# Attention on one core: score and output tiles made in pairs, their matmuls in turn

## What is computed

```
xn = group_norm(x, gamma, beta)              # 16 images, N = 1024 tokens, C = 512
q = xn @ wq + bq;  k = xn @ wk + bk;  v = xn @ wv + bv
scores = einsum('bnc,bmc->bnm', q, k) * C ** -0.5
attn = softmax(scores)
out = einsum('bnm,bmc->bnc', attn, v) @ wp + bp + x
```

## Time and profile before

| | |
|---|---|
| median of 3 runs | 2161.06 us (2159.78 to 2163.63) |
| profiled execution | 2159.59 us, of which the trace's span is 2157.9 us |
| TensorE matmul busy | 2137.5 us, 99%, 9425 instructions |
| TensorE weight loads | 1765.7 us, 82% |
| VectorE / ScalarE / POOL busy | 1454.1 (67%) / 673.8 (31%) / 826.9 us (38%) |
| mean granted TensorE clock | 0.997 |
| DMA | 106.03 MB, 49 GB/s |

### The profile page before, as it was taken

How to read it: one execution, slowest core, us unless ns; L and a number is a source line. 1 busy time by engine, 2 the same in 40 slices (tenths; PEclk the granted TensorE clock), 3 DMA queues, 4 the chain that set the end, 5 groups by cost and what they waited for, 6 DMA issues and landing times.

```text
span 2157.9 us, 28171 instructions
## 1 busy us (share of the span) xinstructions
PE 2137.5 (99%) x9425; PEld 1765.7 (82%) x9425; DVE 1454.1 (67%) x2280; ACT 673.8 (31%) x1113; POOL 826.9 (38%) x487
## 2 busy tenths in 40 slices
PE   7999999999999999999999999999999999999998
PEld 5888888888888888888888888888888888888886
DVE  6776675857768476784856758576684767847454
ACT  3241332414233132331413324142331323314231
POOL 4344343433433334333443434334333343324433
PEclk9999999999999999999999999999999999999999
DMA  7003021130302103021030210303021030210201
GB/s 171 20 16 102 1 74 44 34 83 0 97 20 58 58 5 102 10 63 53 10 107 0 73 44 32 85 0 96 21 58 59 5 102 10 63 53 10 69 0 59
DMA packets 109260, 106.03 MB, mean 49 GB/s; under 512 B 8493, under 2 KB 74033, under 8 KB 109233
## 3 DMA queue, kind: packets, MB, share of 16 engines
q1 hardware_dynamic: 109184, 105.68, 17.4%
q10 hardware_dynamic: 48, 0.01, 0.0%
HBM read 72.10 MB, written 33.55 MB: 49 GB/s over the span
## 4 chain that ended last, share of the span: by engine, by line
PE 96%; POOL 1%; SPq 1%; issue 1%; DMA 1%; DVE 0%; ACT 0%; DVEq 0%; POOLq 0%; ACTq 0%
PE psum L790 21%; PE psum L792 21%; PE psum L791 21%; PE psum L873 11%; PE psum L874 11%; PE psum L875 11%; SPq L236 1%; DMA w_p<-in_L_conv_wp_dram 1%; POOL bias_part L372 0%; SPq L251 0%; POOL out_bias L376 0%; PE psum L836 0%; POOL out_bias L378 0%; DVE pt_lo L526 0%; ACT wv_t_hi L471 0%
## 5 line engine op out<-in xcount | busy, mean ns | idle before, releaser
L873 PE MATMUL psum<-v_hi,pt_hi 128*128 128x512 f32 x1024 | 400.0, 391 | 2.6 <-DVE pt_lo L526 2.5
L790 PE MATMUL psum<-t_hi,xn_hi 128*128 128x512 f32 x1024 | 399.9, 391 | 0.4 <-DVE v_lo L526 0.4
L874 PE MATMUL psum<-v_lo,pt_hi 128*128 128x512 f32 x1024 | 399.3, 390 | 0.0
L875 PE MATMUL psum<-v_hi,pt_lo 128*128 128x512 f32 x1024 | 399.2, 390 | 0.0
L792 PE MATMUL psum<-t_hi,xn_lo 128*128 128x512 f32 x1024 | 398.5, 389 | 0.0
L791 PE MATMUL psum<-t_lo,xn_hi 128*128 128x512 f32 x1024 | 398.5, 389 | 0.0
L324 POOL TENSOR_TENSOR x_res<-x_res,out_bias 128x512 f32<-128x512 f32 (+1 forms) x144 | 181.6, 1271 | 419.7 <-issue 232.0
L618 DVE TENSOR_TENSOR top_part<-top_part,score 128x512 f32<-128x512 f32 x192 | 169.6, 883 | 235.4 <-ACT score L453 234.1
L346 POOL TENSOR_TENSOR total_part<-total_part,score 128x512 f32<-128x512 f32 x192 | 280.7, 1462 | 47.4 <-ACT score L458 32.8
L453 ACT ACTIVATE score<-psum 128x512 f32<-128x512 f32 x256 | 151.5, 600 | 460.8 <-PE psum L792 460.8
L458 ACT ACTIVATE score<-score 128x512 f32<-128x512 f32 x256 | 157.9, 633 | 305.0 <-DVE score L634 305.0
(11 more groups left out here) (101 smaller groups left out, 3004.3 us busy)
## 6 DMA issues: line engine op xcount, KB each, us to landing
x_res<-in_x_dram SPq DMA_DIRECT2D x128, 256.0 KB, 2.8
out_dram<-x_res SPq DMA_DIRECT2D x128, 256.0 KB, 2.1
x_blk<-in_x_dram SPq DMA_DIRECT2D x240, 128.0 KB, 2.9
score<-in_x_dram SPq DMA_DIRECT2D x16, 128.0 KB, 7.6
w_q<-in_L_conv_wq_dram SPq DMA_DIRECT2D x4, 256.0 KB, 4.3
w_k<-in_L_conv_wk_dram SPq DMA_DIRECT2D x4, 256.0 KB, 7.0
w_v<-in_L_conv_wv_dram SPq DMA_DIRECT2D x4, 256.0 KB, 7.9
w_p<-in_L_conv_wp_dram SPq DMA_DIRECT2D x1, 1024.0 KB, 11.0
```

Source lines behind the costliest of these rows:

```text
L790: nc.tensor.matmul(dst, s_hi_, m_hi_, start=n == 0, stop=False)
L873: nc.tensor.matmul(dst, pt_hi[:, m, queries], v_hi[:, m, :], start=m == 0, stop=False)
L874: nc.tensor.matmul(dst, pt_hi[:, m, queries], v_lo[:, m, :], start=False, stop=False)
L875: last = nc.tensor.matmul(dst, pt_lo[:, m, queries], v_hi[:, m, :], start=False, stop=m == NT - 1)
```

## The change

Score tiles m and m + 1 are made together, and so are output tiles i and i + 1. Within a pair each matmul of the one is followed by the same matmul of the other: same moving operand, other weights, other bank. Both banks are waited for ahead of the pair's first matmul, and one signal after its last reports both tiles. An output pair waits for the `tile_out` that frees its second bank. The second group sum still stands behind s(1,1). Nothing changes on the other engines.

```diff
@@ -792,6 +792,17 @@
                     last = nc.tensor.matmul(dst, s_lo_, m_hi_, start=False, stop=n == len(pairs) - 1)
                 return last
 
+            def two_products(dsts, pairs):
+
+                steps = len(pairs[0])
+                for n in range(steps):
+                    for parts in range(3):
+                        for dst, own in zip(dsts, pairs):
+                            s_hi_, s_lo_, m_hi_, m_lo_ = own[n]
+                            last = nc.tensor.matmul(dst, s_lo_ if parts == 2 else s_hi_, m_lo_ if parts == 1 else m_hi_,
+                                                    start=n == 0 and parts == 0, stop=n == steps - 1 and parts == 2)
+                return last
+
             def chunk(c):
                 return slice(c * P, (c + 1) * P)
 
@@ -846,34 +857,34 @@
                 product(dst, [(xn_hi[:, k, chunk(m)], xn_lo[:, k, chunk(m)], m_hi[:, k, :], m_lo[:, k, :])
                               for k in range(KC)]).then_inc(s_work, 1)
 
-            def score_tile(n, h, m):
+            def score_tiles(n, h, m):
                 if m == 0:
 
                     pe.wait_ge(s_free, n * SPLIT + PLACE[("t", h, KC - 1)] + 1)
-                dst = work_bank(n, "s", h, m)
-                product(dst, [(xn_hi[:, k, chunk(m)], xn_lo[:, k, chunk(m)], t_hi[:, k, :], t_lo[:, k, :])
-                              for k in range(KC)]).then_inc(s_work, 1)
-
-            def out_tile(n, i, more):
+                dsts = [work_bank(n, "s", h, m), work_bank(n, "s", h, m + 1)]
+                two_products(dsts, [[(xn_hi[:, k, chunk(c)], xn_lo[:, k, chunk(c)], t_hi[:, k, :], t_lo[:, k, :])
+                                     for k in range(KC)] for c in (m, m + 1)]).then_inc(s_work, 2)
+
+            def out_tiles(n, i, more):
                 h = i // TH
                 if i == 0:
 
                     pe.wait_ge(s_free, (n + 1) * SPLIT)
                 if i >= TH or not starts(n):
 
-                    pe.wait_ge(s_y, n * NT + i - TH + 1)
-                if i == TH - 1 and more:
+                    pe.wait_ge(s_y, n * NT + i + 1 - TH + 1)
+                if i == TH - 2 and more:
 
                     pe.wait_ge(s_pw_in, n + 2)
-                dst = o_ps[i % TH]
                 for m in range(NT):
                     if i % TH == 0:
                         pe.wait_ge(s_ptl, (n * NH + h) * NT + m + 1)
-                    queries = chunk(i % TH)
-                    nc.tensor.matmul(dst, pt_hi[:, m, queries], v_hi[:, m, :], start=m == 0, stop=False)
-                    nc.tensor.matmul(dst, pt_hi[:, m, queries], v_lo[:, m, :], start=False, stop=False)
-                    last = nc.tensor.matmul(dst, pt_lo[:, m, queries], v_hi[:, m, :], start=False, stop=m == NT - 1)
-                last.then_inc(s_o, 1)
+                    for weights, moving in ((pt_hi, v_hi), (pt_hi, v_lo), (pt_lo, v_hi)):
+                        for c in (i, i + 1):
+                            last = nc.tensor.matmul(o_ps[c % TH], weights[:, m, chunk(c % TH)], moving[:, m, :],
+                                                    start=m == 0 and moving is v_hi and weights is pt_hi,
+                                                    stop=m == NT - 1 and weights is pt_lo)
+                last.then_inc(s_o, 2)
 
             pe.wait_ge(s_const, 6)
             weight_transpose(SET_WQ, w_q, s_wload[0])
@@ -898,8 +909,8 @@
             def image(b, more):
                 v_tile(b, 0)
                 v_tile(b, 1)
-                for m in range(NT):
-                    score_tile(b, 0, m)
+                for m in range(0, NT, 2):
+                    score_tiles(b, 0, m)
                 for j in range(KC):
                     t_chunk(b, 1, j)
                 for m in range(2, NT):
@@ -907,17 +918,17 @@
                     if more:
                         if m == 3:
                             group_sum(b + 1, 0, mv[:, :, 0])
-                for m in range(NT):
-                    score_tile(b, 1, m)
-                    if more and m == 1:
+                for m in range(0, NT, 2):
+                    score_tiles(b, 1, m)
+                    if more and m == 0:
                         group_sum(b + 1, 1, dev[:])
-                for i in range(TH):
-                    out_tile(b, i, more)
+                for i in range(0, TH, 2):
+                    out_tiles(b, i, more)
                 if more:
                     for j in range(KC):
                         t_chunk(b + 1, 0, j)
-                for i in range(TH, NT):
-                    out_tile(b, i, more)
+                for i in range(TH, NT, 2):
+                    out_tiles(b, i, more)
 
             if B > 1:
                 image(0, True)
```

## The result

The changed kernel takes 2221.0 us (median of four runs, 2219.78 to 2222.61) against 2160.56 us (also of four runs, one more than above): 60 us more, ratio 1.0281, 95% interval 1.027 to 1.0293. The forecast was 2206.6 us in a range of 2190 to 2232. The sign, the main cause and the range held; 14 us were missing from the sum, and the measured time lies above the 2216 us at which the forecast's own cases end.

The account below looks back on a forecast made before the run. TensorE was taken to bound the kernel, moved only by matmul spacing or a new wait. 34.2 + 2 + 0.2 + 1.1 + 8 = 45.5 us on the 2161.06 us median gave 2206.6 us, range 2190 to 2232.

Parts of the forecast that it names:

- The sign: Whole kernel: the change makes it slower, 2.1%; chances slower 0.90, same 0.04, faster 0.06.
- the main cause: Second half's first score pair: TensorE waits for v5's split once per image, 34.2 us in all.
- the forecast's own cases: The forecast alone, chance 0.6: from 2195 us (stop of 34 us, no fall of the clock) to 2216 us (11 falls).
- Rival 2: TensorE's clock falls at nearly every stop: 2224 us, more if it lasts; chance 0.19.
- Rival 4: The chain ahead slips by more, POOL's all-reduce a us later than now in each image: 2222 us; chance 0.07.
- The spacing: Paired matmuls on TensorE: alternating banks changes nothing, 0 us; they stay 0.227 us apart; bound on the good side 82 us.
- The stop before s(1,0): Second half's first score pair: TensorE waits for v5's split, 2.0 to 2.3 us once per image, 34.2 us.
- The chain ahead of it: First half's last scores arrive together, POOL's all-reduce moves, VectorE's shift is 0 to 0.5 us late per image: 2 us.
- The second pair: Second half's second score pair, needing v7's split: covered by 0.28 us, about 0.2 us lost in the last image.
- The edits costed at nothing: Other score pairs, output pairs, pt_lo use, VectorE's queue, stores and reloads: waits hidden or covered, 0 us.
- The end: Last image after its last scores: POOL's later residuals release the last three tile_outs, the last starting 1.1 us later.
- The clock: TensorE's clock falls after the stop in 5 of 16 images, 1.6 us each: 8 us, bounds 0 and 26.

Follow-up runs that it names:

- report late: Kernel before, but score tiles m and m+1 are both reported at the end of m+1; matmuls and waits as before: 2165.84 us, ratio 1.0021.
- pairs where covered: Changed kernel, but s0 to s3 of each half made one by one and quarter 2 transposed after the maximum of s5: 2162.62 us, ratio 1.0006.
- the three on the last image: Kernel before with, in the last image, output tiles 4 to 7 paired (2159.51 us), also POOL's residuals before its last reduction (2160.13), or those residuals alone (2163.64).
- the run with the wait alone: Kernel before, but TensorE waits for the banks of two score tiles ahead of each even one; order and reports as before: 2198.73 us, ratio 1.0174.

## Why the prediction held, and where it was short

The cause was forecast rightly; that 2221.0 us lies in the range is partly luck. The range reached beyond 2216 us only to take in rivals 2 and 4, and their times, 2224 and 2222 us, were met by other causes than theirs.

**The spacing.** Right, and shown: no change of spacing in the trace, none in the time with outputs alone, with the old order inside the pairs, or with 4608 matmuls alternating where nothing waits. The row at the tile boundary had the answer, since a change of bank was already in it. What the 0.013 us beyond the 512 columns are stays open; it isn't the accumulation into the same bank. (the earlier trace rows are read a little too well: a 9 stands for 90% or more, and the mean granted clock was 0.997.)

**The stop before s(1,0).** Right in place, releaser and number; too small in size. The sum had 34.2 + 2 us for it and it cost 46.1 (44.3 + 1.8). The step that fell short is "The chain ahead of it": I moved POOL's all-reduce by 1.9 us and asked only whether the shift would wait for it. That much was correct: maxima and all-reduce moved so, the shift by 0 to 0.2 us. But POOL has more in its list behind the all-reduce. Its additions moved too, further onto VectorE's two-input steps, and the eight subtractions took 8.90 us instead of 7.99. Rival 4 (the chain slips by more) has the right size, 0.7 us per image, with the wrong mechanism: the chain doesn't start later, it runs slower.

**The second pair.** Right: there is no stop in the trace, in no image; 0.2 us had been put down for the last.

**The edits costed at nothing.** Right for the outputs (1.0003 with them alone). Wrong in one place: "the other score pairs follow ones whose banks were evicted" is false for s(0,2), s(0,3) of image 0. There ScalarE starts v0's hi part only when POOL has finished out_bias, so the splits of v0 and v1 are late. I had read image 7 and taken it for all. TensorE stopped there for 0.5 us in the trace of before and stops for 2.5 in that of the changed kernel, but only 0.6 us of it, the distance from v0's split to v1's, is the pair's doing. The rest differs between executions: in the six runs whose s(0,2) waits for v0 alone (outputs only, report late, pairs where covered, and the three on the last image) the stop is 1.5 to 2.5 us, and in two of those the clock falls behind it. In the run with pairs in the last image alone:

```profile
74.49 0.50 PE L790 MATMUL psum<-t_hi,xn_hi 128*128 128x512 f32 x1 [1.98 <-DVE v_lo L526]
```

So of the 6.0 us of image 0 in the table, up to 3 us may be there without any pair.

**The end.** 1.1 us forecast, 0.35 measured. The last three tile_outs now wait for POOL's residuals, as forecast; in the kernel before the very last one still waited for TensorE. The shift came 1.6 us later, but POOL's last residuals only 0.9 (46.93 us behind the start of the outputs, against 45.99).

**The clock.** Forecast 5 falls at 1.6 us, 8 us; in images 1 to 14 six falls at 1.65, 9.9 us, and two more in image 0, 14 us in all. The price came from the earlier trace rows and was right; the count was a guess between bounds. Rival 2 (nearly every stop) gave 2224 us, close to the time, but for a wrong reason: seven of the images 0 to 14 have a fall, and longer stops make up the difference. The Trainium skill ("TensorE: Matmul & The Clock Gate", A second HAM failure mode: psum-queue depth-cycling) says that idle times between matmul groups while banks are cycled make the clock swing. The trace agrees in kind, but with fewer swings than stops, six in the 14 images from 1 to 14. The length of the stop didn't decide by itself: at 2.37 us the clock fell, at 2.83 it did not, and in the run with the wait alone it fell at one stop of 2.09 us and held at two others of that length.

## What to carry to other kernels

Joining two tiles moves two signals: the second tile's bank is needed one tile earlier, and the first tile's result is reported one tile later. Both have to be followed through every queue, to the engines that only come later in the same list, and in the first pass of a loop as well as in a middle one. A bank that is freed 0.65 us ahead of its need looks like slack and is a 2 us stop once its need moves by 2.7. Before paying for an order of matmuls that is to make them faster, look for a row in the old trace where that order already occurs.

## What the hardware showed that I had not expected

- Two-input VectorE steps on SBUF (L634, 128x512) take 0.68 us alone and up to 1.87 us beside POOL's tensor additions; the split with one input in PSUM stays at 0.69. Twice, a POOL list that merely ran at another time cost TensorE time: 13 us of stops here, and about 2 us with POOL's residuals moved.
- A single stop of 2.4 to 3.5 us in 131 us of dense work is enough for the clock to fall in some cases, and 1.65 us is lost each time. Filling the stop with ten useless matmuls saved 13.5 us.
- The spacing of 128x512 matmuls in this kernel is 0.2267 us whatever changes from one to the next: the moving operand, the weights, or the weights and the bank, as in the pairs. At the lower clock it is 0.427.
